# GpSimd issues its indirect DMAs in rows of four and waits for each row to land

## What is computed

```
def _L0_ffn_ref(...):                       # 16 experts, 4 for each token
    probs = softmax(hidden_states @ router_w + router_b)
    topw, topi = top_k(probs, 4); topw = topw / sum(topw)
    out = sum over the token's 4 experts of topw * (gelu(x @ w1[e] + b1[e]) @ w2[e] + b2[e])
def _L1_ffn_ref(...):                       # 8 experts, 1 for each token
    expert = argmax(probs)
    out = (relu(tokens @ W1[expert] + b1) @ W2[expert] + b2) * max_prob
x = x + _L0_ffn_ref(_layernorm(x), ...)
...
x = x + _L1_ffn_ref(_layernorm(x), ...)
```

## Time and profile before

| what | us |
|---|---|
| timed runs, median (lowest to highest) | 939.73 (938.42 to 946.98) |
| profiled execution, span from first to last instruction | 1010.3 |
| TensorE busy | 728.8 (72%) |
| VectorE busy | 587.4 (58%) |
| ScalarE busy | 355.3 (35%) |
| GpSimd busy | 252.8 (25%) |

### The profile page before, as it was taken

One profiled execution on the slowest core, in us unless ns is written; L12 is line 12 of the kernel. 1 busy time (PEld: TensorE's weight loads), 2 busy tenths in 40 slices (PEclk: granted clock), 3 DMA queues, 4 the chain that ended last, 5 costly groups with the idle time before them and its releaser, 6 DMA issues.

```text
span 1010.3 us, 13395 instructions
## 1 busy us (share of the span) xinstructions
PE 728.8 (72%) x3910; PEld 460.4 (46%) x3910; DVE 587.4 (58%) x2022; ACT 355.3 (35%) x634; POOL 252.8 (25%) x304
## 2 busy tenths in 40 slices
PE   2677763858839665677674766859886678699998
PEld 1223322748838422222374654556664333345555
DVE  6666654427214444466444455979986666576764
ACT  6355420524415223433332322213332466432231
POOL 2140566430342371611306141221110110000000
PEclk9999765969959857866987867988998899799999
DMA  7272022333533340207023100010220121000000
GB/s 175 65 266 66 29 86 78 114 105 95 154 88 88 113 104 16 73 1 249 21 62 99 42 20 1 0 71 1 53 71 1 47 64 32 0 1 11 11 11 12
DMA packets 71218, 65.55 MB, mean 65 GB/s; under 512 B 8996, under 2 KB 62941, under 8 KB 70634
## 3 DMA queue, kind: packets, MB, share of 16 engines
q1 hardware_dynamic: 53610, 48.02, 16.2%
q0 software_dynamic: 5120, 10.50, 3.5%
q10 hardware_dynamic: 12416, 6.16, 2.1%
HBM read 35.61 MB, written 22.94 MB: 58 GB/s over the span
## 4 chain that ended last, share of the span: by engine, by line
PE 40%; issue 22%; DVE 20%; SPq 5%; ACT 4%; another core or an unknown queue 3%; DMA 2%; POOL 2%; ACTq 1%; DVEq 0%
PE psum_all L801 3%; PE psum_all L889 3%; PE psum_all L905 3%; PE psum_all L696 3%; PE psum_all L783 3%; DVE s_nmx L1320 3%; PE psum_all L785 3%; PE psum_all L672 2%; PE psum_all L674 2%; DVE s_h L1462 2%; PE psum_all L653 2%; PE psum_all L613 1%; PE psum_all L978 1%; PE psum_all L771 1%
## 5 line engine op out<-in xcount | busy, mean ns | idle before, releaser
L1320 DVE TENSOR_REDUCE s_nmx<-psum_all 128x4 f32<-128x308 f32 x192 | 83.4, 473 | 59.1 <-PE psum_all L653 36.9
L2518 POOL TENSOR_SCALAR s_vare<-s_mv 128x4 f32<-128x4 f32 x40 | 11.4, 285 | 424.3 <-DVE s_mv L1207 413.3
L2092 ACT ACTIVATE s_hT<-psum_all 77x1024 f32<-77x1024 f32 x96 | 95.9, 1018 | 51.4 <-PE psum_all L674 40.6
L653 PE MATMUL psum_all<-s_ks,s_t 128*128 128x308 bf16 x192 | 60.2, 361 | 48.3 <-DVE s_nmx L1320 26.3
L672 PE MATMUL psum_all<-s_t,s_ks 128*77 128x512 bf16 x192 | 83.8, 437 | 12.8 <-ACT s_hT L2092 9.0
L674 PE MATMUL psum_all<-s_t,s_ks 128*77 128x512 bf16 x192 | 82.4, 429 | 0.0
L2438 POOL DMA_INDIRECT s_w<-routed_y,s_cT x64 | 61.8, 966 | 73.2 <-issue 72.3
L1582 DVE COPY s_t<-s_arena 128x256 f32 x94 | 21.6, 292 | 98.4 <-remote 48.6
L696 PE MATMUL psum_all<-s_hT,s_v 77*32 77x512 f32 x384 | 58.6, 684 | 25.8 <-ACT s_hT L2092 20.7
L905 PE MATMUL psum_all<-s_arena,s_hT 128*128 x376 | 60.4, 295 | 22.6 <-issue 21.6
L2424 POOL DMA_INDIRECT routed_x<-s_x_normed,s_cT x64 | 62.5, 976 | 50.5 <-DVE s_cT L1521 32.2
(11 more groups left out here) (311 smaller groups left out, 1521.8 us busy)
## 6 DMA issues: line engine op xcount, KB each, us to landing
s_t<-q_parts SPq DMA_DIRECT2D x66, 128.0 KB, 2.8
routed_y<-s_hT ACTq DMA_DIRECT2D x22, 256.0 KB
s_ks<-s_att SPq DMA_DIRECT2D x72, 77.0 KB, 2.1
q_parts<-s_qparts SPq DMA_DIRECT2D x11, 384.0 KB
s_arena<-in_w SPq DMA_DIRECT2D x2, 2048.0 KB, 10.2
s_h<-routed_x SPq DMA_DIRECT2D x48, 64.0 KB
s_x_normed<-routed_x SPq DMA_DIRECT2D x46, 64.0 KB
routed_x<-s_w SPq DMA_DIRECT2D x34, 64.0 KB
```

The costliest lines, as they stand in the source:

```text
L653: pe.matmul(o, T1[:, u % QS, g, 128 * i:128 * i + 128], KS1[:, HPG * g:HPG * g + HPG, SK * b:SK * b + SK], start=True, stop=True))
L1320: read(job, dve.tensor_reduce(nmx[:, u % 2, i, HPG * g:HPG * g + HPG], PS[:, k, 0:HPG * SK].rearrange("p (h s) -> p h s", h=HPG), AX.X, AL ...
L2092: read(("S", L, b, p), nc.scalar.activation(Eexp[:, (PAIRS * u + p) % ES, :, :], PS[0:SK, k:k + 2, :], ACT.Exp))
```

## The change

After every fourth indirect DMA of a block (x = 3, 7, 11, 15), and after the fourth of the eight of a half in the sorted layer, POOL waits until this DMA and all earlier ones on its semaphore have landed. No DMA is added, removed or moved, and no other engine's instructions change. There are 16 new waits in the routed scatters, 16 in the routed gathers and 4 in the sorted layer.

```diff
@@ def routed_scatter(b, some): @@
                     pool.indirect_dma_start(RXD[b // 2], bass.IndirectOffsetOnAxis(ap=r_slot_x[:, b, x:x + 1], axis=0),
                                             XN[:, TPB * b + x // TOPK, :], None).then_inc(s_rsc[b], 16)
+                    if x % 4 == 3:
+                        pool.wait_ge(s_rsc[b], 16 * (x + 1))
@@ def routed_gather(b, some): @@
                                             bass.IndirectOffsetOnAxis(ap=r_slot_y[:, b, x:x + 1], axis=0)).then_inc(s_rga[2 * b + x // 8], 16)
+                    if x % 4 == 3:
+                        pool.wait_ge(s_rga[2 * b + x // 8], 16 * (x % 8 + 1))
@@ def scatter(h): @@
                                             XN[:, HT_TILES * h + i, :], None).then_inc(s_sc[h], 16)
+                    if i == 3:
+                        pool.wait_ge(s_sc[h], 16 * (i + 1))
@@ def gather(h): @@
                                             bass.IndirectOffsetOnAxis(ap=slot_of[:, h, i:i + 1], axis=0)).then_inc(s_ga[2 * h + i // TPB], 16)
+                    if i == 3:
+                        pool.wait_ge(s_ga[2 * h], 16 * (i + 1))
```

## The result

| | kernel before | changed kernel |
|---|---|---|
| timed, median (lowest to highest) | 940.93 us (938.42 to 946.98), 4 runs | 959.31 us (957.69 to 965.86), 4 runs |
| ratio after / before, 95% interval | | 1.0192 [1.0149, 1.0235] |
| span of the profiled execution | 1010.3 us | 958.3 us |

The change costs 18.4 us; 22 were predicted. At the same time the profiled span is 52 us shorter. The two don't fit together, and the experiments show why: the execution profiled before had something that slowed it and that those timed runs did not have. That trace is therefore no base for reading where the 18 us went. I use a second profile of the unchanged kernel, whose own time agrees with its timed runs (first experiment).

The account below looks back on a forecast made before the run. POOL's issue was taken to bound the start of the expert layer, TensorE a long stretch behind it. Terms 8 + 2 + 0 + 0 + 3 + 3 + 1 + 5 = 22 us on 939.7 gave 962 us; 8-in-10 range 934 to 983.

Parts of the forecast that it names:

- Start of the expert layer: Routed scatters up to block 1's last landing: 7 new waits at 1.20 us, bounds 4.7 and 8.4, taken as 8.
- The 20 gathers from block 0 on: Gathers beside the second half's quads: 5 waits, 10 us, hidden, only a later norm behind them; cost 0.
- Norm of block 3: Norm on POOL behind scatters of blocks 1 and 2, two further waits, POOL idle 4.33 us before: 0 to 2.4, taken 2.
- The other gathers: 12 gathers of block 1, 22 of blocks 2 and 3, last 10, partly hidden by POOL's idle time: 3 + 3 + 1 us.
- Sorted layer: One wait a half in each of two directions, all four count: 6.6 us, one gather may hide: 5.
- The base: The 22 us are added to the timed median of 939.7 us, not to the profiled span of 1010.3.
- the crawl: Twelve stretches behind indirect DMA bursts where engines but POOL nearly stop: roughly 75 us, read as belonging to the recorded execution.
- Rival A: Crawl is real and also in the timed runs, rows of four remove much of it: 905 us (880 to 930), chance 0.18.
- Price of a wait: Added POOL time per new wait if nothing is hidden: scatter 1.20 us, gather 2.09 us; 59 us upper bound.
- The 0.14 for a restart: Part of each wait's price: the first DMA behind a pause takes 1.10 us instead of 0.96.
- Scatters of blocks 2 and 3: 7 more waits after block 3's norm, 8.4 us, hidden behind 12 quads of TensorE: 0; without that cover 8.
- What was to show it: Changed profile: POOL gaps near 1.4 and 2.2 us, slow SP register moves rare, TensorE busier behind bursts, span well below 1010.

Follow-up runs that it names:

- first experiment: Kernel before, unchanged, profiled and timed again: 943.49 us (10 runs), ratio 0.9972, profiled span 942.2 us.
- the group of runs on the slower chip: Against kernel before (1018.12 us), waits only in scatters of blocks 2 and 3: 0.9849; first 20 gathers: 0.9851, with later combine 0.9830; other 44 gathers: 0.9862.

## Why the prediction came out, and where its steps failed

The forecast was 22 us for waits on the way of POOL's bursts; 18.4 and 17.0 us were measured. One of its larger terms held (the start, 8), one large one was missing (the first gathers, 7.4 by the timed runs), and several that came out smaller stood in for it (norm of block 3, the other gathers and the sorted layer, 14 together, of which the runs show some 1 to 4). The start is understood; that the sum lands within 4 us of the time is in good part luck.

**The base: right number, wrong reason.** I wrote that the crawl belongs to the recorded execution, because its cost (75 us) equals the excess over the timed runs (70.6). The equality was real: the crawl is that excess. The cause was not. The record does not name the chip of the first profile, so that it ran on another one than the timed runs is inferred, not shown: the medians of the kernel before are 941 to 945 us in four groups of runs and 1018 in one, and traces show the crawl only where the time is long. A second profile could have told. The rule that I had cited from the Trainium skill (Runtime: NRT & Kernel Launch, preamble and postamble: profile total and reported time differ by about 6.2 us whatever the kernel) was right against me in kind: recording did not make an execution 70 us longer. In every later profiled execution the span lies 1.8 to 1.9 us below that execution's own time (942.2 and 944.05, 958.3 and 960.08, 1003.8 and 1005.63). This is not the page's 6.2, which is an excess of a profile total over the time; the span here runs from the first to the last instruction, and no run shows that total.

**Rival A: true on some chips.** Its core, that the crawl is in timed runs and rows of four end it, holds on the chip with 1018 us, where each of three parts of the change saves some 15 us, the cost of the waits already taken off. My argument against it, that a register move has no reason to wait for a DMA, only said that I knew no reason. Its 905 us did not follow: it took the crawl off a time that had none in it.

**Price of a wait: right to some 0.3 us in light stretches.** In light stretches a scatter's wait is 1.55 - 0.30 = 1.25 (1.20 predicted), in the loaded stretch of blocks 2 and 3 up to 2.5 - 0.30 = 2.2. A gather's is on average 27.1 / 13 - 0.30 = 1.8 (2.09 predicted), up to 3.0 - 0.30 = 2.7 in this trace. The 0.14 for a restart was wrong as a rule: most DMAs behind a wait take 0.94 to 0.96, as the others do, and a few up to 1.13. The Trainium skill's 2.0 us for such a DMA (DMA: Bandwidth & Descriptors, anatomy of a DMA), heaviest towards HBM, lies above the scatters' wait of 1.55 and near the gathers' mean of 2.1, both counted from the end of POOL's instruction. The order of the two is the other way round here too; a gather's wait also holds its read from DRAM, which no run separates.

**Start of the expert layer, 8: right.** The way from the first scatter to the first gather grew by 6.9, 8.0 and 8.2 in three traces over the second profile of before, whose 131.1 is the shortest of five; timed alone 5.5 [2.5, 8.5].

**Norm of block 3, 2: it was 0.** See the three equal rows above. I read POOL's idle time of 4.33 as the reserve; what decided was VectorE, whose copy for TensorE stands ahead of its part of the norm, not the norm's place on POOL.

**Scatters of blocks 2 and 3, 0: consistent.** They were not run alone without the crawl, but the traces with all waits have no longer way to the first gather (138.0, 139.1) than that with waits in blocks 0 and 1 alone (139.3).

**The 20 gathers from block 0 on, 0: the failed step.** I wrote that behind them "stands only a norm that comes later". In the first profile the crawl stretched everything up to that norm (51.8 us), so it seemed far away. Without the crawl POOL reached it 25.1 us after the first gather, only 2.4 ahead of VectorE's statistics, and five waits of some 1.8 are 9: 2.4 hidden, 6.6 left. Beside it VectorE's second combine, which the statistics of the norm follow, needs the last gathers of block 0 and came 4.4 to 6.4 us later after the first gather in the traces with these waits. Measured +6.6 to +8.4 in the traces that keep the order of the DMAs, +7.4 timed. I had allowed for crawl inside an idle time on POOL for block 1 and for blocks 2 and 3, and had not asked the same question here.

**The other gathers, 7: about 0.** They were not timed alone without the crawl; all gathers together cost 8.1, the first 20 alone 7.4, and the fourth stretch is no longer with waits (104.8 to 105.9) than without (102.5 to 108.9). Without the crawl POOL still waits 8.71 us ahead of norm (2,1) and 12.16 ahead of norm (2,2):

```profile
296.50 0.23 POOL L2518 TENSOR_SCALAR s_vare<-s_mv 128x4 f32<-128x4 f32 x1 [8.71 <-DVE s_mv L1207]
...
341.18 0.23 POOL L2518 TENSOR_SCALAR s_vare<-s_mv 128x4 f32<-128x4 f32 x1 [12.16 <-DVE s_mv L1207]
```

These answer 13.17 and 21.27 in the earlier trace rows. In the changed kernel the second is still there by a hair (0.59 us ahead of norm (2,2)); the waits used up the reserve and stopped short of the end:

```profile
350.83 0.23 POOL L2526 TENSOR_SCALAR s_vare<-s_mv 128x4 f32<-128x4 f32 x1 [0.59 <-DVE s_mv L1207]
```

I had estimated that reserve at 6 by taking 15 us of crawl off the idle time.

**Sorted layer, 5: too large.** The traces give 3 to 4, the timed runs at most 2.2.

**What was to show it.** Gaps of 1.4 and 2.2, no slow register moves, a span between 940 and 985: all came true, but the last two say nothing about the change, since the kernel before has no crawl either where these runs were timed (940.93). Three signs that I had called a test of "rows of four end the crawl" would have passed without it. The test was the group of runs on the slower chip.

**Still open.** What the whole change does on the slower chip was not measured, as no later group ran on one. An estimate from the table, adding for each stretch the kernel that has its waits there (111 + 140 + 34 + 107 + 573), gives 965 us of span, against 1010: rows of four would then be worth 4% there and cost 2% elsewhere. It leaves out the waits that no run tried on that chip, those in the scatters of blocks 0 and 1 and in the sorted layer. What the crawl is, also stays open. The queue of the indirect DMAs (packets, MB, share of the 16 DMA engines' time), in the crawl of 273 to 296 us of the first profile, and in a burst without one, 241 to 266 us of the second:

```profile
q0 software_dynamic: 545, 1.12, 18.4%
```

```profile
q0 software_dynamic: 599, 1.25, 18.5%
```

The same load at the same speed: it is not the volume that these DMAs move.

## What to carry to other kernels

Before a trace is used as a price list, hold its span against the timed runs; where they differ by more than their scatter, profile the same kernel again rather than explain the gap, and look for the difference in an instruction that should depend on nothing, such as a register move. A reserve read from a disturbed stretch is no reserve: ask of every idle time that hides a cost what it would be without the disturbance, also where the cost was put at nothing. When two engines meet a delay at different places, find the one whose arrival is late: moving the work of the others only moves the wait. And look for a second path to the same place that is late for the same reason, as VectorE's was beside POOL's.

## What the hardware showed beyond what I expected

The same program took 942 to 945 us (medians) on three chips and 1018 us on another one, each run within 1.1% of its median over 11 to 29 runs. Each chip was used for one group of runs only, so a lasting trait of the chip and a passing condition are not told apart. In the first profile the excess lies in stretches behind some four or more indirect DMAs issued by POOL in a row, in which every other engine slows down: SP's register moves from 29 to as much as 717 ns, and TensorE is busy for 11.49 of 30 us where it is for 26.09 with rows of four. Only POOL goes on as before (0.96 us a DMA). A wait for landing after every fourth DMA ended it in each of three stretches that were tried. On the other chips a burst of 20 in a row did nothing of the kind: in the second profile of before TensorE is busy for 28.91 of the 30 us from 240 on.
